# Order of work around the probabilities in a cross-attention kernel: high halves, low halves, weight slots, and the last batch

## What is computed

```python
# layer 0: 16 heads of 32, key mask, then an MLP (512 -> 2048 -> 512, tanh gelu)
x = x + attention(layer_norm(x), ctx) @ cproj + b
x = x + mlp(layer_norm(x))
# layer 1, twice (a = 0, 1) with weights of its own: 16 heads of 128 (inner width 2048)
kh = concat([ctx @ wk + bk, bias_k])       # 375 keys and one extra key
vh = concat([ctx @ wv + bv, bias_v])
p = softmax(qh @ kh.T / sqrt(128))
x = x + (p @ vh) @ wo + bo
# and an MLP (512 -> 2048 -> 512, exact gelu)
```

## Time and profile before

| | |
|---|---|
| median of 3 runs | 2407.84 us (2407.47 to 2410.53) |
| the profiled execution, its own time | 2412.1 us |
| its span, first to last instruction | 2409.9 us |
| mean granted TensorE clock | 0.979 |
| busy: TensorE, weight load, DVE, ACT, POOL | 2258.8, 2027.3, 1384.3, 1116.7, 609.1 us |
| attention of layer 1, a = 0 and a = 1 | about 545 to 1285 and 1445 to 2180 us |

### The profile page before, as it was taken

The page is one execution under the profiler, slowest core; times in us unless marked ns, Lnnn a source line. Parts: engine busy times, 40 slices in busy tenths (PEclk is TensorE's granted clock), DMA queues, the critical chain, the costliest instruction groups (busy, mean ns, idle before and its releaser), DMA issues.

```text
span 2409.9 us, 36258 instructions
## 1 busy us (share of the span) xinstructions
PE 2258.8 (94%) x12323; PEld 2027.3 (84%) x12323; DVE 1384.3 (57%) x3102; ACT 1116.7 (46%) x2276; POOL 609.1 (25%) x919
## 2 busy tenths in 40 slices
PE   7999999997999999999988998999998998988999
PEld 6777788897998888898887897988888898977888
DVE  6877863515665665665653525665665565553843
ACT  5777742533444444444433543444444444443421
POOL 2111074401222222222222301222222223122421
PEclk9999999999999999999999999999999999999999
DMA  6322156646877877877864647787887887765110
GB/s 200 120 86 99 62 162 194 211 158 217 276 262 226 274 258 227 273 261 226 277 201 127 211 162 221 255 271 240 259 266 241 263 271 237 236 189 160 57 53 31
DMA packets 326902, 483.18 MB, mean 200 GB/s; under 512 B 65726, under 2 KB 250962, under 8 KB 324674
## 3 DMA queue, kind: packets, MB, share of 16 engines
q1 hardware_dynamic: 326722, 480.87, 61.9%
HBM read 370.30 MB, written 110.49 MB: 200 GB/s over the span
## 4 chain that ended last, share of the span: by engine, by line
PE 67%; DVE 10%; POOL 6%; ACT 6%; issue 6%; DMA 4%; SPq 1%; DVEq 0%; ACTq 0%; POOLq 0%
PE ps_o L1820 7%; PE ps_o L1822 6%; PE ps_o L1821 6%; PE ps_v L1820 5%; PE ps_v L1822 5%; PE ps_v L1821 5%; POOL pt_lo L912 5%; PE ps_k L1820 5%; PE ps_k L1821 4%; PE ps_k L1822 4%; PE ps_s L1820 3%; PE ps_s L1822 3%; PE ps_s L1821 3%; DMA turned_probabilities<-blocks 3%; PE ps_t L1821 2%
## 5 line engine op out<-in xcount | busy, mean ns | idle before, releaser
L1207 ACT ACTIVATE prob<-ps_s,row_columns 128x376 f32<-128x376 f32 x256 | 147.1, 575 | 378.0 <-DVE row_columns L1600 377.9
L912 POOL TENSOR_TENSOR pt_lo<-pt_lo,pt_hi 128x512 fp32r<-128x512 f32 x192 | 245.3, 1307 | 227.2 <-ACT pt_hi L1183 227.2
L904 POOL CAST k_hi<-xk_hi 128x1 fp32r<-128x1 f32 x256 | 52.8, 206 | 895.5 <-PE ps_s L1822 895.5
L1820 PE MATMUL ps_v<-pt_hi,ckd 128*128 128x448 f32 (+1 forms) x384 | 155.1, 404 | 81.4 <-POOL pt_lo L912 63.0
L1820 PE MATMUL ps_k<-cs_hi,w_a_hi 128*128 128x376 f32 x636 | 219.5, 345 | 0.0
L1821 PE MATMUL ps_k<-cs_lo,w_a_hi 128*128 128x376 f32 x636 | 214.7, 338 | 0.0
L1822 PE MATMUL ps_k<-cs_hi,w_a_lo 128*128 128x376 f32 x636 | 213.2, 335 | 0.0
L859 POOL TENSOR_TENSOR w_b_lo<-w_raw_b,w_b_hi 128x512 fp32r<-128x512 f32 x80 | 109.3, 1391 | 349.4 <-ACT w_b_hi L963 349.3
L1616 DVE STREAM_TRANSPOSE blocks<-prob 128x384 f32<-128x384 f32 x256 | 148.1, 579 | 68.4 <-DMA turned_probabilities<-blocks 60.3
L1488 DVE TENSOR_SCALAR prob<-prob,row_columns 128x375 f32<-128x375 f32 (+1 forms) x384 | 177.4, 462 | 4.5
L1485 DVE RECIPROCAL row_columns<-row_columns 128x1 f32<-128x1 f32 (+1 forms) x384 | 62.5, 163 | 196.1 <-ACT prob L1207 188.5
(11 more groups left out here) (290 smaller groups left out, 6391.8 us busy)
## 6 DMA issues: line engine op xcount, KB each, us to landing
ckd<-context_by_key_halves SPq DMA_DIRECT2D x256, 384.0 KB, 5.1
turned_probabilities<-blocks SPq DMA_DIRECT2D x64, 768.0 KB, 3.8
pt_lo<-turned_probabilities SPq DMA_DIRECT2D x256, 192.0 KB, 4.0
cs_hi<-context_halves SPq DMA_DIRECT2D x64, 752.0 KB, 5.8
cs_lo<-context_halves SPq DMA_DIRECT2D x64, 752.0 KB, 7.4
w_raw_b<-in_blocks_b SPq DMA_DIRECT2D x104, 256.0 KB, 3.5
w_raw_a<-in_blocks_a SPq DMA_DIRECT2D x104, 256.0 KB, 4.1
q<-q_scratch SPq DMA_DIRECT2D x64, 256.0 KB, 3.6
```

The costliest lines, as they stand in the source:

```text
L912: pool.tensor_tensor(lo, lo.bitcast(F32), hi, ALU.subtract).then_inc(t_lo, 1)
L1207: act.activation(prob[buf][:, 0:KW], ps_s[buf][:, 0:KW], ACT.Exp, bias=max_neg[:, buf:buf + 1], accum_out=prob_sum[:, buf:buf + 1]).then_i ...
L1820: pe.matmul(out, w_h, m_h, start=first, stop=False)
```

## The change

1. ACT's `turned_hi` moves ahead of the step's exponential. POOL makes the low halves in the order of the key blocks (four runs of 128 columns each instead of 512 in a row), and the first sum waits for one block at a time.
2. ACT's and POOL's halves of slot b move from t = 0, 1 to t = 2, 3 of b = 2. SP's loads move from b = 2, t = 1 to b = 3: slot a at t = 0, slot b at t = 1. Query pieces are stored behind the other transfers of their step.
3. The head outputs alternate between the banks ps_o[0] and ps_t[1], in every group, and a product waits for the output before last. The last one is no longer done in halves.
4. In the last batch of a layer the probabilities are neither stored nor turned by DVE. TensorE turns each head (`last_turned`, three transposes into one bank), ACT copies the high half out of the bank into pt_hi, and DVE subtracts the low half into pt_lo. At t = 2 the step has the quarters 0, 1 and 2 of b = 6 with the turns of heads 2 and 3 between them, at t = 3 the quarter 3.
5. The two early row tiles are projected in `project`, ahead of the other five, instead of in the epilogue. The engines' epilogues follow that order.

The diff, cut to its core (new semaphores and the counters that follow from the batch that is left out are not shown):

```diff
@@ class Place
+        self.fetches = isinstance(self.b, int) and self.b == 3 and att.layer and group > 0
-        return {0: (0, 1), 1: (2, 3)}.get(t, ()) if self.att.layer and self.loads else ()
+        return {2: (0, 1), 3: (2, 3)}.get(t, ()) if self.att.layer and self.loads else ()
@@ chunks
+            if place.final and t >= 2:
+                return {2: ((last, 0), (last, 1), (last, 2)), 3: ((last, 3),)}[t]
@@ helpers
+        def last_bank(t):
+            return (ps_t[1], ps_k, ps_t[0], ps_t[1])[t]
+        def key_tile(part, place, j):
+            return pt[place.parity][part][:].rearrange("p (i j f) -> p j i f", i=BANDS, j=3)[:, j]
         def final_bank(place, t):
-            return (ps_o[0], ps_s[0], ps_s[1], ps_t[1])[t] if place.final else ps_o[0]
+            return (ps_o[0], ps_t[1])[t % 2]
         def y_bank(layer, group, r):
-            return (ps_k, ps_t[0])[r] if layer and group == 0 and r < EARLY_TILES else ps_y[r % 4]
+            return ps_y[r % 4]
@@ SP one_batch
-                        if query_piece(place, t):
-                            last_query(query, a, skip, query_piece(place, t))
...
                         if t == 2:
                             store_extra(place)
-                            store_blocks(place)
+                            if not place.final:
+                                store_blocks(place)
                         if t == 3:
-                            load_turned(place)
+                            if not place.final:
+                                load_turned(place)
...
                             load_by_key(summed.next(), d)
-                        if t == 1 and place.loads:
+                        if query_piece(place, t):
+                            last_query(query, a, skip, query_piece(place, t))
+                        if t == 0 and place.fetches:
+                            load_block(0, place.block_a + 1)
+                        if t == 1 and place.fetches:
                             load_block(1, place.block_b + 1)
-                            load_block(0, place.block_a + 1)
@@ POOL turned_lo
-                    for i in range(3):
-                        part = slice(i * D, (i + 1) * D)
-                        hi, lo = (pt[place.parity][s][:, part] for s in range(2))
+                    for j in range(3):
+                        hi, lo = (key_tile(s, place, j) for s in range(2))
@@ ACT
+                def last_turned_hi(place, t):
+                    act.wait_ge(last_turn, NT * a + t + 1)
+                    if t == 0:
+                        act.wait_ge(c_mm, NT * place.visit - NT)
+                    act.activation(last_place(0, place, t), last_turned(t), ACT.Identity).then_inc(last_hi, 1)
@@ ACT one_batch
                             sum_hi(summed, d)
+                            if place.final and t == 2 and d < 2:
+                                last_turned_hi(place, d + 2)
+                        if t == 0 and place.before():
+                            turned_hi(place.before())
+                        if place.final and t < 2:
+                            last_turned_hi(place, t)
                         if place.key(t + 2):
                             exp(*place.key(t + 2))
-                        if t == 0 and place.before():
-                            turned_hi(place.before())
@@ DVE normalized_1, one_batch
+                    if place.final:
+                        return
...
+                            if place.final and t == 2 and d < 2:
+                                last_turned_lo(place, d + 2)
+                        if place.final and t < 2:
+                            last_turned_lo(place, t)
                         if place.key(t + 2):
                             maximum(*place.key(t + 2))
@@ PE
+                def last_turned(place, t):
+                    pe.wait_ge(s_norm, place.unit + t + 1)
+                    if t == 3:
+                        pe.wait_ge(last_lo, NT * a + 1)
+                    for j, (k0, n) in enumerate(KEY_TILES):
+                        last = pe.transpose(last_bank(t)[0:n, j * P:(j + 1) * P], prob[t % 2][:, k0:k0 + n], ident[:])
+                    last.then_inc(last_turn, 1)
@@ PE context_sum
-                    if d == 0:
-                        pe.wait_ge(t_lo, 3 * place.visit + 3)
+                    if d == 0 and place.final:
+                        pe.wait_ge(last_lo, NT * a + NT)
...
                     for i in range(3):
+                        if d == 0 and not place.final:
+                            pe.wait_ge(t_lo, 3 * turned_batches(place) + i + 1)
@@ PE head_output
-                        wait(pe, z_ev, NT * place.quads + (0 if place.final else t))
+                    wait(pe, z_ev, NT * place.quads + max(t - 1, 0))
@@ PE epilogue
-                    for d in (2, 3):
-                        context_sum(place.before(), d)
-                    pe.wait_ge(w_lo[0], 4 * (place.block_a + 1) + 4)
-                    pe.wait_ge(early_lo, a + 1)
-                    for r in range(EARLY_TILES):
-                        project_row(1, 0, 0, 5 * RT + 4 * RT * a, r, early)
                     for d in range(DT):
                         context_sum(place, d)
-                    for part in ((0, 2), (2, DT)):
-                        for t in range(NT):
-                            head_output(place, t, part)
+                    for t in range(NT):
+                        head_output(place, t)
@@ PE project
-                for r in range(EARLY_TILES if group == 0 else 0, RT):
-                    pe.wait_ge(p_lo, 3 * (GROUPS * a + group) + CHUNK_OF[r] + 1)
+                for r in range(RT):
+                    from_early = group == 0 and r < EARLY_TILES
+                    if from_early:
+                        pe.wait_ge(early_lo, a + 1)
+                    else:
+                        pe.wait_ge(p_lo, 3 * (GROUPS * a + group) + CHUNK_OF[r] + 1)
```

89 lines of the change are left out of this document (49 added, 40 removed).

## The result

Median of the changed kernel 2345.72 us in four runs (2336.15 to 2350.98), of the kernel before beside it 2409.19; ratio 0.973, interval 0.9697 to 0.9764. Faster, as forecast, and inside the range, but 25 us above the forecast of 2321 and near the upper end of the range: 63 us were won where 86.5 had been added up. In a later comparison the same kernel gave 2334.67 against 2404.0, ratio 0.9705 (0.9685 to 0.9725), 13.7 us above the forecast.

What follows compares the result with a forecast made beforehand. TensorE, busy 94%, bounds the kernel; its waits and low clock form a 150 us pool. Seven terms sum to 86.5 off the profiled 2412.1, giving 2325.6; with the median 4.3 below the profile, 2321 us; range 2282 to 2352.

Steps and rivals of the forecast that it cites:

- the pool: TensorE's waits plus its time at the low clock in the two layers of 128-wide heads: 150 us to win.
- Part 3: At b=2, weight halves move to t=2, 3; the 2.14 us gaps go: saves 20 us, bounds 13 and 21.
- part 6: Layer start: query store behind the turned load, which goes out earlier; saves 12 us, bounds 6 and 15.
- part 7: Layer end: TensorE turns the last batch, without store and load; saves 24 us, bounds 14 and 31.
- Part 2: At b=7, ACT's and DVE's queues move up by 0.6 us, six times: saves 3.6 us, bounds 0 and 11.
- part 1: Ordinary batches: high halves before the exponential, low halves by key block; saves 5.9 us, load cover 1.2 us.
- rival E: ACT at t=0: turned load later than the high halves' new place in every batch, slower than before; chance 0.04.
- Part 4: Weight loads at t=0 and t=1 of b=3, blocks store pushed back 0.8 us: saves 15, bounds +48 and -12.
- Rival D: b=3/b=4 no better than today, or the layer ends at their lower bounds: 2336 to 2350 us; chance 0.15.
- Part 5: Two banks for value products remove 27 short waits for DVE's o: saves 6 us, bounds 0 and 6.9.
- Rival C: Shared DVE/POOL port: the t=0 normalise meets a whole low half, 0.8 us in some 48 batches: 2358; chance 0.10.
- Rival B: The loads of b=3 are covered after all, so that place saves 48 us: 2288 us; chance 0.18.

Runs made afterwards that it cites:

- x5: Changed kernel with SP storing the last query pieces ahead of the turned load again: 2345.54 us, ratio 0.975 to the kernel before.
- x7: Kernel before with parts 1 to 6 of the change and without part 7: 2355.77 us, ratio 0.9799 to the kernel before.
- x8: Changed kernel with the weight column halves at t=0 and t=1 of b=7 moved to t=1 and t=2: 2316.65 us, ratio 0.964.
- x1b: Changed kernel with ACT's high halves behind the exponential again, except in the last batch of a layer: 2319.59 us, ratio 0.9647.
- x6: Changed kernel with all head outputs in one bank again, each waiting for the one before: 2352.03 us, ratio 0.9788.
- x3: Changed kernel with the slot b weight load issued one column each at t=1 of b=3, 4, 5 and 6: 2327.47 us, ratio 0.9681.
- x4: Changed kernel with weight halves back at t=0, 1 of b=2 and both weight loads at t=1 of b=2: 2343.19 us, ratio 0.9751.
- the repeat: The changed kernel itself, unaltered, timed again beside the follow-up runs: 2334.67 us, ratio 0.9705 to the kernel before.

## Why the prediction was right in sign and too large in size

The sign, the pool and the three large parts (3, 6, 7) were right; two terms were wrong by 8 us each. That the total still came near is in part luck: by place the errors are -18.7 us (ordinary batches 2.3, b=7 8.1, b=3 and b=4 8.3) and +8.1 us (b=2, the starts, the ends and the 0.4), and they cancel in part.

- **The pool and the ends.** The reading that 150 us of waits and low clock in the two layers are all that can be won held: 75.9 us were won, and all but 0.4 of them there. Part 3 (20, measured 21.9 in place), part 6 (12, measured 15.0, and 11 by x5) and part 7 (24, measured 26.8, and 23 by x7) were each within 3 us of their terms. Of the late exponentials that I charged to part 7 one wait of 0.68 us is to be seen, and the 1.5 us a layer by which q's low half was to cut part 6 did not show: each start gave 7.2 to 7.8.
- **Part 2, wrong in sign.** "I take only the 0.6 by which ACT's and DVE's queues move up: 3.6." Measured -4.5. The queues didn't move up. The load landed 0.96 us after ACT wanted it, the exponential stood behind 1.49 us of high halves, and the chain from the maximum to the scores stayed at some 9 us while TensorE came to its end 2 us earlier. The forecast had both pieces: "DVE is the bound here", and a cover of 1.2 us "and if it is gone the exponential waits too". It never put the two together in the one batch kind where the chain of DVE has least idle time. And it had no term for the low clock, which three of the six waits brought. x8 shows the weight column in the chain as one cause (16 us with the clock, all at b=7), x1b the order of the exponential as the other (some 5 of its 14 us lie at b=7).
- **The cover of part 1.** There was none in the old trace either. The forecast put the landing at 1.74 us of issues plus the 4.0 us of the last line of the earlier trace rows, 606.3. But 4.0 is the median of a single issue, and ACT waits for the last of four; the view of the load in the kernel before:

```profile
DMA to landing us min/median/max: 2.8/4.0/6.5
```

  From the first issue to the last landing the 64 loads took 5.6 to 7.9 us, and the one of 600.54 took 6.95, so it landed at 607.49, when the new order wants it (607.5). In 24 of the 64 batches the old trace has less than the 1.66 us by which the high halves were to move. Part 6 used 6.9 us for the same load. Measured: 34 waits and 52.9 us. They have the place that rival E names, and they meet the sign that was set for it, pt_hi waiting for DMA in most batches (34 of 62), but mostly by 0.2 to 2.8 us and in every second ordinary batch, so the whole did not become slower. The path exponential, transposes, store (4 to 5 us), load (some 6 us), high halves, exponential is closed through the new order; behind the exponential, as in x1b, the high halves are no part of it, and the waits are gone. That the length of this loop sets the pace is argued.
- **Part 4, a term mis-sized.** 15, measured 6.7. "Each is four issues, 3.03 us ... and so pushes the blocks store back by 0.8 us." It was 3.7 to 4.7 us, since SP's issue of q between the two loads grew from 0.4 to 2.5 us and the extra store from 0.3 to 1.5. That took DVE's wait over the 4.6 us up to which, by the forecast, TensorE doesn't notice. The landing itself was put at 6.0 to 7.0 us and came out at 5.7 to 6.8. Rival D, a b=3/b=4 little better than before, was the nearest to what came.
- **Part 5, priced for the short waits alone.** 6 in the sum; putting one bank back costs 20 us (x6). Of these the trace places 7 in the batches with head outputs, as forecast, and 5.2 at the first end: the ends, where heads follow one another with nothing between them, need the second bank too, and the sum had given that to part 7 unasked.
- **Rival C** did not come: of 384 normalises 51 took 0.5 to 0.9 us before and 67 after, and of the seven that now take more one is in the two layers. POOL's block boundary stayed close to the normalise.
- **Rival B** needed b=3 without a delay; x3 comes nearest and reaches it for k_lo only.
- **The sum of parts.** Put back singly, parts 3 and 4 cost 11 us (x4) where the trace had credited their places with 28.6. The forecast priced the batches in place, so its sum holds, but it can't be read as a price list of edits: the wait by key block and the order depend on each other, and places in the trace on what follows them.
- **Profile and median.** The forecast moved the sum by the 4.3 us that the profile stood above the median before. After the change the profile stood 9.6 below it in the first four runs, and 0.2 in the repeat. A forecast should have had this much room.

## What to carry to other kernels

When a producer with a DMA in front of it is moved ahead of a consumer on an in-order engine, work out the whole loop (store, landing, load, landing, conversion) against the new length of the iteration. If it is about as long, let the consumer wait by parts and leave the order alone. Take the landing of such a load from its first issue to its last landing, and not from the median of one issue. Check the exceptional iteration by itself: putting the exponential first won 14 us in the body and lost about 9 at the ends of the layers. And price a part that gets rid of a wait by where the next producer in the same queue ends, one batch kind at a time.

## What the hardware showed beyond that

The granted clock fell to 1.2 GHz (0.50 in the window above) behind a wait of 1.69 us and stayed at 2.4 GHz behind one of 1.68 at the same place in another execution; the 15 matmuls from there on took 1.5 us longer at the low clock. I counted the waits of TensorE from 545 to 2185 us in all fourteen traces, and those in which the granted clock fell between their start and 2 us behind their end: 2 of 57 for waits of 0.9 to 1.25 us, 34 of 120 for 1.25 to 1.75, 46 of 74 for 1.75 to 2.75, and 41 of 42 for 2.75 to 4.25. So a wait of 1.5 us costs 1.5 us plus, in between one case of four and one of three, about as much again, and shortening it to 1 us wins more than the half microsecond: in x8 the gaps fell by 5.5 us and the cost of the low clock by 9.6.

The second surprise is SP's issue times: one and the same issue, the load of q, took 0.37 us at b=7 and 2.47 us behind a megabyte of weight loads, whose four transfers landed only at 774.5 to 777.6 us. What holds SP there no run here tells apart.
